# The drain of a three-stage image and text kernel, written out by hand: FFN tiles on two and three bank sets, the last pair in groups, and constant matmuls in the gaps

## What is computed

```python
loc  = dwconv(gelu(conv(x, pl_w, stride=16)), pl_dw, pl_pw)          # layer L
g    = gelu(conv(wavelet_packet(x), pg_w1))
glob = conv(gelu(dwconv(g, pg_dw, pg_pw)), pg_w2)                    # layers G, W2
h    = (1 - gate) * loc + gate * glob
h    = relu(dwconv(h, f1));  h = relu(dwconv(h, f2))                 # layers F1, F2
t    = layernorm(dwconv(loc + h, f3))                                # layer F3, 196 tokens
tok  = concat([cls, t, txt])                                         # 325 tokens an image
q, k, v = (mlp(layernorm(tok), w) for w in (qw, kw, vw))             # two linear layers with gelu
y    = tok + layernorm(band_mask(q @ k.T) @ v)                       # a span of 64 tokens
u, w = split(bitlinear(y, w_in));  z = gate_act(w) * u               # ternary weights, 8 bit activations
out  = y + bitlinear(z, w_out)
```

## Time and profile before

| | |
|---|---|
| median of 3 runs | 1186.11 us (1184.85 to 1186.3) |
| the profiled execution's own time | 1183.86 us |
| its span, first to last instruction | 1182.1 us |
| mean granted TensorE clock | 0.94 |
| busy share of the span | PE 89%, DVE 82%, ACT 75%, POOL 67% |

### The profile page before, as it was taken

One profiled execution on the slowest core, in us unless ns is written; L12 is line 12 of the kernel. 1 busy time (PEld: TensorE's weight loads), 2 busy tenths in 40 slices (PEclk: granted clock), 3 DMA queues, 4 the chain that ended last, 5 costly groups with the idle time before them and its releaser, 6 DMA issues. The chain is left out here.

```text
span 1182.1 us, 18959 instructions
## 1 busy us (share of the span) xinstructions
PE 1056.5 (89%) x5594; PEld 701.3 (59%) x5594; DVE 968.8 (82%) x2799; ACT 883.8 (75%) x2179; POOL 796.2 (67%) x913
## 2 busy tenths in 40 slices
PE   6886999999999999999999999999999877868434
PEld 4664676767666666767575757576766545444211
DVE  1678778989999999999898989899999976754543
ACT  4455767898979797979798988889897856654433
POOL 4246467778787878777877877787878755653422
PEclk9797999999999999999999999999999988979655
DMA  8111010101010101011010101010100000000000
GB/s 331 42 48 41 1 49 3 52 9 59 10 59 7 58 4 64 4 28 41 19 49 12 55 10 59 10 58 11 58 10 18 10 16 5 23 4 17 4 19 15
DMA packets 23686, 41.14 MB, mean 35 GB/s; under 512 B 3648, under 2 KB 20384, under 8 KB 21280
## 3 DMA queue, kind: packets, MB, share of 16 engines
q1 hardware_dynamic: 23584, 39.93, 10.0%
HBM read 31.02 MB, written 7.99 MB: 33 GB/s over the span
## 5 line engine op out<-in xcount | busy, mean ns | idle before, releaser
L1359 DVE SCALAR_TENSOR_TENSOR bank<-padA,c_col,bank 128x406 f32<-128x406 f32 x560 | 358.6, 640 | 9.1
L496 PE MATMUL bank<-x_sb,w_emb 128*128 128x392 f32 x576 | 221.3, 513 | 5.4 <-ACT padA L903 3.1
L953 ACT ACTIVATE prod<-padB,c_col 128x196 f32<-128x196 f32 x432 | 176.5, 451 | 7.2 <-DVE padB L1371 3.9
L1889 POOL TENSOR_TENSOR yg<-y_f,c_gout 128x512 f32<-128x512 f32 (+1 forms) x79 | 100.4, 1271 | 69.2 <-DVE y_f L1544 69.1
L496 PEld LDWEIGHTS bank<-x_sb,w_emb 128*128 128x128 f32 x576 | 102.5, 195 | 63.0 <-issue 12.8
L953 ACT ACTIVATE early<-padB,c_col 128x196 f32<-128x196 f32 x288 | 118.8, 449 | 3.7 <-POOL accB L1923 3.6
L1524 DVE SCALAR_TENSOR_TENSOR ya<-th,bank 128x512 f32<-128x512 f32 (+1 forms) x79 | 54.1, 684 | 56.4 <-ACT th L1022 55.2
L638 PE MATMUL bank<-w_in,xq 128*128 128x512 bf16 (+1 forms) x316 | 86.6, 399 | 8.8 <-ACT xq L1016 8.8
L1010 ACT ACTIVATE yq<-bank 128x512 bf16<-128x512 f16 (+1 forms) x79 | 46.8, 592 | 48.4 <-PE bank L648 47.2
L474 PE MATMUL bank<-accA,w_sq 128*128 128x196 f32 x256 | 67.6, 346 | 10.9 <-POOL accB L1923 6.8
L1022 ACT ACTIVATE th<-bank,sm 128x512 f32<-128x512 f32 (+1 forms) x79 | 53.7, 680 | 29.0 <-PE bank L638 29.0
(11 more groups left out here) (276 smaller groups left out, 3030.9 us busy)
## 6 DMA issues: line engine op xcount, KB each, us to landing
x_sb<-xt SPq DMA_DIRECT2D x16, 1176.0 KB, 5.2
out<-o_sb SPq DMA_DIRECT2D x64, 96.0 KB
w_sq<-squares SPq DMA_DIRECT2D x1, 3840.0 KB, 16.4
h_sb<-txt SPq DMA_DIRECT2D x32, 51.8 KB
out<-o_sb SPq DMA_DIRECT2D x32, 48.0 KB
h_sb<-txt SPq DMA_DIRECT2D x32, 44.2 KB
w_in<-win SPq DMA_DIRECT2D x1, 1024.0 KB, 17.6
h<-h SPq DMA_DIRECT2D x16, 48.0 KB, 1.9
```

Source lines behind the costliest of these rows:

```text
L496: done = mm(pE[:, 0:2 * N_PATCH], w_emb[:, k, m, :], x_sb[:, k, :], start=k == 0, stop=k == KC - 1)
L953: made = go(grid(prod[ACC[s] ^ 1][:, k, :]), tap_view(padB[min(s, 2)], SIDE, k), ACT.Copy, scale=tapcol(s, 1, k))
L1359: v.scalar_tensor_tensor(grid(acc if k == TAPS - 1 else run), tap_view(pad, ROWS_A, k), tapcol(s, 0, k), grid(run), ALU.mult, ALU.add).the ...
L1889: g.tensor_tensor(ygs[s][0:m, :], yfs[s][0:m, :], c_gout[0:m, :], ALU.mult).then_inc(f_yg, 1)
```

## The change

It has five parts.

1. *The drain is written out.* DVE and POOL run the turns 0 to 15 as before, PE, ACT and SP the turns 0 to 16, and then each runs a list of its own, `drain()`, of 422, 151, 220, 288 and 34 calls. They hold the calls of the left-out turns in another order. In general the convolution layers of pairs 14 and 15 stand earlier and the FFN tiles of pairs 11 and 12 later than before.
2. *Sides.* From pair 13 on (`tail`) FFN tiles alternate between (`pUP`, `pGT`) and (`pA`, `pB`); the last pair's go round three sets, the third being attention's (`pT`). Scratch for the second set lies in `x_sb` and `w_emb`, for the third in `hq`, `hk`, `hv`, `k2`, `xh` and `xT`. A tile's token transposes now wait until the tile before on its own side is finished (`side_before`), and for nothing of the other side.
3. *Three output buffers* and three scale columns (`dq2`) in place of two, in all pairs.
4. *The last pair in groups.* Its output norm, FFN statistics and scales are taken in three groups of two tiles. Centering, gain and the residual add, which were one operation on ACT and two wide ones on POOL for each pair, are two DVE operations per tile here; POOL keeps the roots, by group.
5. *Constant matmuls.* `keep_busy(n)` on PE issues n matmuls of 512 columns of the ternary weights into `pE`, which nothing reads after the last embedding. 41 such calls issue 97.

```diff
-def side(f, n):
-    return n % 2 if last(f) else 0
+TAIL = PAIRS - 3
+def side(f, n):
+    if last(f):
+        return (n + 1) % 3
+    return (tile_no(f, n) - tile_no(TAIL, 0) + 1) % 2 if tail(f) else 0
...
-        ups, gts = [pUP, pA], [pGT, pB]
+        ups, gts = [pUP, pA, pT[0]], [pGT, pB, pT[1]]
...
             def rounded_token_transposes(f, n):
                 pe.wait_ge(r1_ready, tile_no(f, n) + 1)
-                if not (first(f) and n == 0 or alone(f, n)):
-                    pe.wait_ge(f_y, tile_no(f, n) * 2)
-                if not (first(f) and n < 2 or last(f) and n == 1):
-                    pe.wait_ge(f_out, tile_no(f, n) - 1)
+                if tail(f):
+                    if side_before(f, n):
+                        pe.wait_ge(f_out, side_before(f, n))
+                    elif side(f, n) == 1:
+                        pe.wait_ge(z_step, (PAIRS - 1) * 4 + 1)
+                    else:
+                        pe.wait_ge(at_act, PAIRS * ACT_UNITS)
...
+            def keep_busy(n):
+                for _ in range(n):
+                    mm(pE[:, :], w_in[:, 0, 0:P], w_in[:, 0, 0:HID], start=True, stop=True)
...
+            def last_output(f, par, j):
+                dve.wait_ge(l_root, j + 1)
+                for n in tiles_in(OUT_GROUPS[j]):
+                    done = v.scalar_tensor_tensor(y_sb[0:m, n, :], y_sb[0:m, n, :], nm_y[0:m, n:n + 1],
+                                                  row("attn_ln_w", m), ALU.add, ALU.mult)
+                done.then_inc(l_y, 1)
+                dve.wait_ge(l_y, j + 1)
+                for n in tiles_in(OUT_GROUPS[j]):
+                    done = v.scalar_tensor_tensor(h2[par][0:m, n, :], y_sb[0:m, n, :], rs_y[0:m, n:n + 1],
+                                                  hb_sb[0:m, n, :], ALU.mult, ALU.add)
+                done.then_inc(l_h2, 1)
...
+            def drain():            # PE, from the tile (14, 1) to the end of (15, 0)
...
+                ffn_in(14, 2)
+                keep_busy(14)
+                rounded_hidden_transposes(14, 1)
+                keep_busy(2)
+                ffn_out(14, 1)
+                keep_busy(2)
+                rounded_token_transposes(14, 3)
+                keep_busy(1)
+                ffn_in(14, 3)
...
+                rounded_token_transposes(15, 0)
+                rounded_token_transposes(15, 1)
+                ffn_in(15, 0)
+                ffn_in(15, 1)
+                rounded_hidden_transposes(*last_tile(14))
...
+            def drain():            # DVE, around the last taps
...
+                taps(15, F3_, 8)
+                hidden_round(0, 12, 0, 0)
+                finished(*last_tile(11))
...
+                gated(12, 1)
+                lifted(12, 1)
+                token_biased(15, 0)
+                token_biased(15, 1)
...
-            all_turns(turn)
+            all_turns(turn, 16)
+            drain()
```

More of the change, by code:

```diff
@@ L116, in stores_before, with tail, side_before @@
 def stores_before(g, parity):
-    return 16 * sum(stores_of(*TILE_LIST[i]) for i in range(parity, g, 2))
+    return 16 * sum(stores_of(*TILE_LIST[i]) for i in range(parity, g, OUTS))
+TAIL = PAIRS - 3
+def tail(f):
+    return f >= TAIL
 def side(f, n):
-    return n % 2 if last(f) else 0
-def alone(f, n):
-    return last(f) and n > 0
+    if last(f):
+        return (n + 1) % 3
+    return (tile_no(f, n) - tile_no(TAIL, 0) + 1) % 2 if tail(f) else 0
+def side_before(f, n):
+    return max((i + 1 for i in range(tile_no(f, n)) if side(*TILE_LIST[i]) == side(f, n)), default=0)
 def build(nc, xt, txt, cls, squares, f3w, v2w, plw, w1w, haar, cols, broads, gout, win, wout, mask,
@@ L373, in build, with all_turns @@
         N_ZERO = len(FILL)
-        def all_turns(turn):
-            for it in range(PAIRS + DEPTH - 1):
+        def all_turns(turn, stop):
+            for it in range(stop):
                 turn(it, it % 2, [0 <= it - k < PAIRS for k in range(DEPTH)])
@@ L460, in _ @@
             sp.wait_ge(s_zero, N_ZERO)
-            all_turns(turn)
-            for parity in range(2):
+            all_turns(turn, 17)
+            drain()
+            for parity in range(OUTS):
                 sp.wait_ge(stored[parity], stores_before(len(TILE_LIST), parity))
@@ L633, in ffn_in @@
                 pe.wait_ge(f_xq, tile_no(f, n) + 1)
-                if not (first(f) and n < 2 or alone(f, n)):
+                if not (first(f) and n < 2 or tail(f)):
                     pe.wait_ge(f_yq, tile_no(f, n) - 1)
@@ L654, in ffn_out @@
                 pe.wait_ge(f_yq, tile_no(f, n) + 1)
-                if not (first(f) and n == 0 or alone(f, n)):
+                if not (first(f) and n == 0 or tail(f)):
                     pe.wait_ge(f_out, tile_no(f, n))
@@ L1693, in turn @@
                 if on[5]:
-                    token_gain(it - 5, odd, range(0, 3))
+                    if not last(it - 5):
+                        token_gain(it - 5, odd, range(0, 3))
+                    if last(it - 5):
+                        last_gain(it - 5, odd, 0)
+                    if last(it - 5):
+                        last_scale_1(it - 5, odd, 0)
                 if on[3]:
```

1326 lines of the change are left out of this document (1292 added, 34 removed).

## The result

| | before | after |
|---|---|---|
| median | 1185.48 us (4 runs, 1184.0 to 1186.3) | 1143.1 us (4 runs, 1141.89 to 1147.13) |
| profiled execution: time, span | 1183.86, 1182.1 us | 1147.13, 1145.3 us |
| mean granted clock | 0.94 | 0.971 |
| ratio of the medians | | 0.965, 95% interval 0.9623 to 0.9677 |

The change gains 42 us. The forecast was 1111.5 us with a range of 1094 to 1138: right in sign, 31.6 us too low, and 5 us outside the range.

A forecast was written before the change was run, and what follows sets the result against it. The drain was taken as latency-bound, no engine full in the last 219 us. Terms of 982, 60, 61 and 4.5 us gave a span of 1107.5; with 1.8 around it and 2.2 to the median, 1111.5 us, range 1094 to 1138.

The forecast's parts named there:

- from there to the end: From the start of the last `finished` to the end, including the store: 4.5 us, unchanged.
- First leg: To pair 15's last F3 tap: DVE's work and remaining idle time put its end at 982 us, 36 us sooner.
- DVE's wait for a store: In the drain, DVE's one 4.0 us wait behind a store would go with the third output buffer.
- Second leg: From pair 15's last tap to its masked scores: less waiting shortens 77.8 us to 60, not under 51.
- four parts: Tap to token statistics, token norm and add, cls row and input norm, projections to scores: 7.6, 7.1, 11 and 34 us.
- The order costs nothing by itself: Whole drain: rewriting the queues' order was given no cost of its own.
- Third leg: Pair 15's masked scores to the last `finished`: 53 us of DVE work, bank bound 52.5, taken as 61, about 87% full.
- The pace of 5 to 6 us: Sign in the later profile: `gated` of pair 14's tiles every 5 to 6 us.
- Constants: 97 constant matmuls on PE, 0.26 us each at most, 25 us: free where PE would wait, otherwise up to 25.
- The tiles' price of half clock: FFN tiles behind the scores: five in line at 1.2 GHz take 6 us longer.
- Tiles one at a time: Rival, chance 0.20: in-order queues keep tiles about 6.7 us apart, eleven take 74 us rather than 61; 1124 to 1128 us.
- The clock rival: Chance 0.12: TensorE's clock stays down for tiles, perhaps projections and scores, adding 6 and up to 25 us; 1117 to 1143.

The follow-up runs named there:

- control: The changed kernel run once more, unaltered, beside the other kernels on one chip: 1143.91 us, ratio 0.9657.
- join first: Changed kernel with pair 13's join and the text load of pair 15 ahead of tile (11, 5)'s 24 store issues on SP: 1136.71 us, ratio 0.9604.
- a lighter PE: Kernel with the join ahead of the stores, some FFN matmuls of pairs 12 and 13 left out: 1136.87 us.
- the earlier tokens: Kernel with the join ahead of the stores, pair 15's last square layer, token statistics and norm moved earlier in the queues: 1137.53 us.

## Why the prediction was wrong

The dates are those of the profiled executions; a leg ends where the operation named has ended, but the third where the last `finished` begins, as in the forecast.

| leg | forecast | after | after, again (control) | join first |
|---|---|---|---|---|
| to the last tap | 982 | 986.6 | 985.1 | 986.0 |
| tap to masked scores | 60 | 87.8 | 83.8 | 78.5 |
| scores to the start of the last `finished` | 61 | 66.4 | 66.3 | 66.0 |
| from there to the end | 4.5 | 4.4 | 4.4 | 4.4 |
| span | 1107.5 | 1145.3 | 1139.6 | 1134.9 |

**First leg: right.** DVE's sum gave the tap 3 to 5 us too early. DVE's wait for a store is gone, as said, but not by the third buffer: with two buffers there is none either, so the new order did it.

**Second leg: this step failed.** The forecast said "Nothing shortens this chain but less waiting" and counted on less of it: 7.6, 7.1, 11 and 34 us for the four parts. They took 19.6 (to 1006.2), 7.3 (to 1013.5), 24.0 (to 1037.5) and 36.9; with the join first 15.7, 7.3, 18.5 and 37.0. The second is right and the fourth near. The first and third, 18.6 us together in the forecast, took 43.6 and with the join first 34.2: the waits did not shrink as assumed, and those of the first part grew. Three things were left out, all of them orders in a queue that the forecast had at nothing ("The order costs nothing by itself").

One is that pair 15's chain is not the only one. In the trace of before pair 14's scores were masked 21.5 us behind the last tap, at 1039.8 (DVE's timeline of before); now it is 41 us, at 1027.6, and with the join first 31, at 1017.1:

```profile
1039.51 0.28 DVE L1567 SCALAR_TENSOR_TENSOR sc<-bank,r_key,c_mask 69x69 f32<-69x69 f32 x1
```

The list pulled the taps forward by 32 us, pair 14's attention by 12 (23 with the join first), and pair 15 has to wait for it: bringing its token statistics forward by 4.5 us moved nothing. Its scores follow pair 14's by 46.9 us in the changed kernel, 47.2 in the control and 47.5 with the join first, though pair 14's lie 41, 37 and 31 us behind the tap. The forecast read only DVE's room. PE's was in the earlier trace rows: 45.7 of 46.0 us and 41.6 of 50.0 behind 867. That this kept pair 14's attention back is not shown; behind the tap a lighter PE does not help. Which chain of waits holds the two pairs apart is open: six kernels that moved the statistics, the likeliest one, each made a new wait on PE.

The second is the order on POOL and PE ahead of the square layer: it began 8.3 us behind the tap, in the trace of before 1.5. On POOL its last sum stood behind pair 13's two wide operations, on PE the layer itself behind pair 14's third projection and a tile's first matmuls, which ended only 0.20 us before the layer began. This is 6.8 of the first part's 12 us. With the join first it hides behind pair 14's chain: with the earlier tokens the layer began 3.1 us behind the tap, and nothing was gained.

The third is a queue that I did not walk: SP's. The forecast counted stores for the wait that the third buffer removes, not for the 24 issues that the new list puts ahead of a join. That, with the clock behind it, is 9.3 us of the leg against the first profiled execution, 5.3 against the control, and 6 to 7 us of the medians. The 18.5 us by which the leg is longer than forecast even with the join first were not given back by any run.

**Third leg: right in kind, 5.4 us short.** DVE's 53 us of work are what it did (23.2 + 15.0 + 14.8), at 80% instead of 87%. The third set is worth 16 us and the groups 8; both were in the term without a price of their own. The pace of 5 to 6 us for pair 14 was wrong: its tiles come 7.9 us apart in the mean, with the last pair's normalisation between them in DVE's list, and the last pair makes it up at 3.4.

**Constants: free in the gaps, as said,** and all 97 are worth 4 to 5 us. The tiles' price of half clock, 1.2 us each in line for five tiles, was too high: the whole leg lost about 3 us.

**The rivals.** Tiles one at a time is what the last pair does on two sets, at 6.0 us. The clock rival named 1117 to 1143 us, for tiles, projections and scores of pair 15 at half clock. That its upper end is the measured time is luck: projections and scores of pair 15 ran at 1.00, and the low clock, ahead of them, is worth about 4 us. The Trainium skill's "TensorE: Matmul & The Clock Gate", in "A second HAM failure mode: psum-queue depth-cycling", has short pauses between groups of matmuls make the clock swing and cost throughput, in a kernel that pauses in every iteration; the traces agree in kind, with two pauses of 1.5 and 2.1 us and a clock of 0.60 behind them.

## What to carry to other kernels

When an order is rewritten, walk every queue between the step that is moved and the next that needs it, the DMA issuing queue too: 24 small stores are 8 us in which a join cannot start. Before one pair's work is pulled forward, look for the pair ahead of it in the same queues: here the taps came 32 us forward, the attention of the pair ahead 12 to 23, and the last pair's scores followed that. Price a short wait on TensorE with the clock behind it: here constants that hold the clock give back 3.5 to 4.3 of the 6.4 to 7.2 us that a late join costs. The best version found is the changed kernel with the join ahead of those stores, 1136.7 us, 0.9604 of before.

## What the runs showed of the hardware

Two waits of PE of 1.5 and 2.1 us within 4 us went with a granted clock of 0.50 from about 1007.7 to 1024.8, which began in the second wait, while PE was busy 4.0 of 4.0 us from 1014 to 1018 and from 1018 to 1022. In another execution of the same program, with the same waits, it was 0.50 from about 1005.9 to 1012.7. One wait of 2.3 to 2.6 us, and in other kernels one of 2.1, went with 0.50 for 3.4 to 10.2 us; the fall came in the wait or up to 2.7 us behind its end. The same program had 0.67 over 1002 to 1028 in one execution and 0.87 in another, and 4.0 of the 5.7 us between their times lie between the last tap and the scores. Constant matmuls in the two gaps held 1.00. Twenty-four store issues held SP's queue for 8.05 us.
